# Placing edges into cells: counts on two PSUM banks and ahead of the lookups, drains on VectorE in place of its own semaphores

## The reference, cut to what matters

```python
h = jnp.maximum(_layernorm(x, axis=-1), 0.0)
x = x + _L0_gnn_ref(h, edge_index, edge_attr_40, edge_weight, ...)   # gate MLP, then 4 attention layers
h = jnp.maximum(_layernorm(x, axis=-1), 0.0)
x = x + _L1_gnn_ref(h, edge_index)                                   # 5 steps of spreading over the graph

# in _L0_gnn_ref, on every edge, before the layers:
src, dst = (edge_index[0], edge_index[1])
gate = jax.nn.silu(edge_attr @ F1W + F1b) @ F2W + F2b
msg = gate * h[dst] * (cw * mj)[:, None]
agg = jax.ops.segment_sum(msg, src, num_segments=N)
# in each of the 4 layers: score per edge, segment_max, exp, segment_sum over src
```

## Time and profile before

| what | us |
|---|---|
| median of 3 runs (8886.3 to 8914.17) | 8893.32 |
| the profiled execution, its own time | 8881.17 |
| its span, first to last instruction | 8879.4 |
| first and last start of a scatter in placing | 368.2 and 2786.5 |

### The profile page before, as it was taken

One profiled execution on the slowest core, in us unless ns is written; L12 is line 12 of the kernel. 1 busy time (PEld: TensorE's weight loads), 2 busy tenths in 40 slices (PEclk: granted clock), 3 DMA queues, 4 the chain that ended last, 5 costly groups with the idle time before them and its releaser, 6 DMA issues. The chain is left out here.

```text
span 8879.4 us, 294906 instructions
## 1 busy us (share of the span) xinstructions
PE 6921.8 (78%) x143255; PEld 6085.1 (69%) x89873; DVE 5928.4 (67%) x15778; ACT 4764.3 (54%) x15185; POOL 5505.5 (62%) x7877
## 2 busy tenths in 40 slices
PE   4544454445445999998799979998999989997998
PEld 4433333333334888887588858886888778877998
DVE  5555555555556999998688868876888678873111
ACT  0222222222224888886588858885888768881000
POOL 2266666666666666665588858885888678880000
PEclk9866666666667999999799989997999899998999
DMA  9522222222224777776477737772777457754565
GB/s 390 206 75 74 77 77 74 74 79 77 77 71 125 252 252 247 252 252 212 139 235 236 232 104 234 234 229 96 238 233 237 147 185 236 235 189 198 236 255 210
DMA packets 735820, 1616.56 MB, mean 182 GB/s; under 512 B 97576, under 2 KB 427272, under 8 KB 729955
## 3 DMA queue, kind: packets, MB, share of 16 engines
q1 hardware_dynamic: 674798, 1514.15, 50.9%
q0 software_dynamic: 52768, 77.90, 2.8%
q10 hardware_dynamic: 6869, 5.50, 0.2%
HBM read 1177.09 MB, written 420.09 MB: 180 GB/s over the span
## 5 line engine op out<-in xcount | busy, mean ns | idle before, releaser
L2017 ACT ACTIVATE vals<-carry_h,weight 128x49 f32<-128x49 f32 x9604 | 2322.3, 328 | 6.4
L1013 POOL DMA_INDIRECT edge_records<-rec_space,slot_all x1600 | 1583.4, 990 | 1090.4 <-DVE slot_all L996 554.4
L437 PE MATMUL psum<-TT,hd_t 128*128 128x97 bf16 x9604 | 1380.9, 208 | 120.1 <-POOL ts L2133 68.8
L431 PE MATMUL psum<-TT,hd_t 128*128 128x97 bf16 x19208 | 1445.2, 208 | 0.4 <-issue 0.4
L437 PEld LDWEIGHTS psum<-TT,hd_t 128*128 128x128 fp8e4 x9604 | 938.9, 98 | 422.5 <-DVE carry_h L2131 69.7
L2062 POOL TENSOR_TENSOR vals<-vals 128x343 f32<-128x343 f32 x1372 | 1072.1, 781 | 92.8
L2057 POOL TENSOR_TENSOR vals<-vals 128x343 f32<-128x343 f32 x1372 | 1044.9, 762 | 4.8 <-ACT vals L2017 4.7
L772 ACT COPY attr_t<-psum 80x500 f32<-80x500 f32 x200 | 114.3, 572 | 1538.4 <-remote 1320.1
L1922 DVE SCALAR_TENSOR_TENSOR xks<-recs,psum 128x343 f32<-128x343 f32 x1372 | 695.3, 507 | 343.1 <-PE psum L431 334.5
L431 PE MATMUL psum<-ts,hs_t 128*128 128x49 bf16 x19208 | 922.2, 184 | 0.0
L1894 PE MATMUL psum<-vals,hs 128*128 128x147 bf16 x9604 | 872.6, 234 | 23.8 <-POOL vals L2062 23.7
(11 more groups left out here) (360 smaller groups left out, 15477.8 us busy)
## 6 DMA issues: line engine op xcount, KB each, us to landing
AJ<-adjacency SPq DMA_DIRECT2D x35, 5488.0 KB, 16.7
recs<-attributes SPq DMA_DIRECT2D x196, 686.0 KB, 5.5
hs<-one_hots SPq DMA_DIRECT2D x392, 336.0 KB, 3.1
one_hots<-hots SPq DMA_DIRECT2D x343, 336.0 KB, 4.2
edge_records<-zeros SPq DMA_DIRECT2D x49, 2278.5 KB
recs_g<-edge_records SPq DMA_DIRECT2D x343, 325.5 KB, 5.2
recs<-attributes SPq DMA_DIRECT2D x196, 514.5 KB, 3.7
hd_t<-one_hots SPq DMA_DIRECT2D x196, 448.0 KB, 4.7
```

The source lines that it names most:

```text
L431: return e.add_instruction(mybir.InstMatmult(name=nc.get_next_instruction_name(), engine=mybir.EngineType.PE, ldweights=False, start_tenso ...
L437: e.matmul(out, hot, parts[0], start=True, stop=False)
L1013: e.indirect_dma_start(REC[:, :], bass.IndirectOffsetOnAxis(ap=slot_all[:, i % SR, s:s + 1], axis=0), rec_rings[:, (i // 2) % 4, s, i % 2, ...
L2017: last = e.activation(vals[:, c, 0, :], carry_h[:, par(back), c, :], ACT.Copy, scale=weight[:, par(back), c:c + 1])
```

## The change

The counts of cells go to two PSUM banks in turn (bank 3 for even steps, bank 2 for odd ones). `count(i)` waits for `s_based` of one step earlier than before, and `count(i + 2)` stands at the head of PE's step. On DVE six plain drains a step take the place of the waits on its own semaphores; `s_load` is not posted any more in placing, and the other semaphores are posted as before because other engines or SP wait for them. `move_on` no longer waits for its own `s_based`.

```diff
-                hist_ps = bank(3)[:, 0:8 * NB].rearrange("p (q s b) -> p q s b", q=4, s=2)
+                hist_ps = [bank(3 - r)[:, 0:8 * NB].rearrange("p (q s b) -> p q s b", q=4, s=2) for r in range(2)]
...
                     def count(i):
                         e.wait_ge(s_hot, i + 1)
-                        if i:
-                            e.wait_ge(s_based, i)
+                        if i >= 2:
+                            e.wait_ge(s_based, i - 1)
...
                     for i in range(ITER):
+                        if i + 2 < ITER - 1:
+                            count(i + 2)
                         if i + 1 < ITER:
                             find_bases(i + 1)
                         mlp_step(i + LEAD + 1, "flip", READY)
                         mlp_step(i + LEAD, "hide", READY)
-                        if i + 2 < ITER - 1:
-                            count(i + 2)
                         mlp_step(i + LEAD - 1, "multiply", READY)
...
                             e.wait_ge(s_found, i)
-                            e.wait_ge(s_based, i)
...
                     for i in range(ITER):
-                        e.wait_ge(s_rank, i + 1)
                         e.wait_ge(s_found, i + 1)
-                        e.wait_ge(s_hot, i + 1)
+                        e.drain()
...
                         rank_more(2)
-                        e.wait_ge(s_looked, i + 1)
-                        e.tensor_reduce(found[:, :, :], look[:, :, :, :], AX.X, ALU.add).then_inc(s_load, 1)
+                        e.drain()
+                        e.tensor_reduce(found[:, :, :], look[:, :, :, :], AX.X, ALU.add)
                         rank_more(2)
-                        e.wait_ge(s_load, 4 * i + 2)
-                        e.tensor_tensor(slot_m[:, :], rank[:, i % 2, :], found[:, :, 0], ALU.add).then_inc(s_load, 1)
+                        e.drain()
+                        e.tensor_tensor(slot_m[:, :], rank[:, i % 2, :], found[:, :, 0], ALU.add)
                         rank_more(1)
-                        e.wait_ge(s_load, 4 * i + 3)
+                        e.drain()
```

More of the change, by code:

```diff
@@ L870, in count @@
                         e.wait_ge(s_hot, i + 1)
-                        if i:
-                            e.wait_ge(s_based, i)
+                        if i >= 2:
+                            e.wait_ge(s_based, i - 1)
                         for q in range(4):
-                            last = e.matmul(hist_ps[:, q, :, :].rearrange("p s b -> p (s b)"), pair_of(one_bs, i, q), pair_of(one_bd, i, q), start=True, stop=True)
+                            last = e.matmul(hist_ps[i % 2][:, q, :, :].rearrange("p s b -> p (s b)"), pair_of(one_bs, i, q), pair_of(one_bd, i, q), start=True, stop=True)
                         last.then_inc(s_flat, 1)
@@ L939, in rank_stream @@
                             last.then_inc(s_rank, 1)
-                    e.tensor_copy(mask, lower[:, :]).then_inc(s_load, 1)
+                    e.tensor_copy(mask, lower[:, :])
                     make_hots(0)
@@ L949, in move_on @@
                             e.wait_ge(s_found, i)
-                            e.wait_ge(s_based, i)
                         for s in range(2):
                             spot = lambda r: bases[r % 2][64 * s:64 * s + NB, :, s, 0, :]
-                            last = e.tensor_tensor(spot(i + 1), spot(i), hist_ps[64 * s:64 * s + NB, :, s, :], ALU.add)
+                            last = e.tensor_tensor(spot(i + 1), spot(i), hist_ps[i % 2][64 * s:64 * s + NB, :, s, :], ALU.add)
                         last.then_inc(s_based, 1)
@@ L959, in place_edges @@
                     move_on(0)
-                    e.wait_ge(s_load, 1)
+                    e.drain()
                     for s in range(NS):
@@ L979, in place_edges @@
                         rank_more(2)
-                        e.wait_ge(s_looked, i + 1)
-                        e.tensor_reduce(found[:, :, :], look[:, :, :, :], AX.X, ALU.add).then_inc(s_load, 1)
+                        e.drain()
+                        e.tensor_reduce(found[:, :, :], look[:, :, :, :], AX.X, ALU.add)
                         rank_more(2)
-                        e.wait_ge(s_load, 4 * i + 2)
-                        e.tensor_tensor(slot_m[:, :], rank[:, i % 2, :], found[:, :, 0], ALU.add).then_inc(s_load, 1)
+                        e.drain()
+                        e.tensor_tensor(slot_m[:, :], rank[:, i % 2, :], found[:, :, 0], ALU.add)
                         rank_more(1)
-                        e.wait_ge(s_load, 4 * i + 3)
+                        e.drain()
                         e.scalar_tensor_tensor(slot_a[:, :], slot_m[:, :], float(NB), home[:, i % 3, :], ALU.mult, ALU.add)
-                        e.scalar_tensor_tensor(slot_b[:, :], slot_m[:, :], float(1 - NB), found[:, :, 1], ALU.mult, ALU.add).then_inc(s_load, 1)
+                        e.scalar_tensor_tensor(slot_b[:, :], slot_m[:, :], float(1 - NB), found[:, :, 1], ALU.mult, ALU.add)
                         rank_more(1)
-                        e.wait_ge(s_load, 4 * i + 4)
-                        e.scalar_tensor_tensor(slot_b[:, :], slot_m[:, :], float(CAP), slot_b[:, :], ALU.is_ge, ALU.mult).then_inc(s_load, 1)
+                        e.drain()
+                        e.scalar_tensor_tensor(slot_b[:, :], slot_m[:, :], float(CAP), slot_b[:, :], ALU.is_ge, ALU.mult)
                         rank_more(2)
@@ L994, in place_edges @@
                             scattered(i - SR)
-                        e.wait_ge(s_load, 4 * i + 5)
+                        e.drain()
                         e.tensor_tensor(slot_i[:, i % SR, :], slot_a[:, :], slot_b[:, :], ALU.add).then_inc(s_idx, 1)
```

## The result

| | us |
|---|---|
| before, median of 3 (8886.3 to 8914.17) | 8893.32 |
| after, median of 3 (8830.88 to 8839.14) | 8832.68 |
| ratio, 95% interval | 0.9942, 0.9918 to 0.9966 |
| span of the profiled execution, before and after | 8879.4 and 8830.9 |

The account below looks back on a forecast made before the run. POOL's scatters and its pauses for slots were taken to bound placing. Two thirds of steps at 13.2 us and one third at 11.9 gave 2555 us, +136, hence 9030 us; its own range was 8950 to 9130, the overall one from 8740.

Parts of the forecast that it names:

- What bounds the kernel: Placing: POOL's scatters set a floor of 2080 us; the other 340 us are pauses waiting for slots.
- pattern of cycles: Placing: waits are free about 10 us after POOL restarts, then posts crawl until it pauses, commonly after two steps.
- the flush: Placing: all pending posts land together about 3 us after POOL's last scatter.
- Own waits gone: DVE's slot steps in placing: up to 361 us of idle in 173 steps vanish, 2.1 us a step.
- the third slot at 15 to 16 us: DVE's slot for POOL's third step is ready 15 to 16 us after POOL's restart, so POOL goes on after two steps.
- Six drains at 0.15 us: DVE in placing: drains add 0.9 us a step, exposed only in the look-to-slot chain, five drains, 0.75 us.
- The three-step cycle, 39.7 us: POOL in placing: an early third slot makes three-step runs the rule, 13.2 us a step, with a longer pause after.
- Count first, two banks, 0 with 40 us to either side: PE's count in placing, moved first with two banks: worth 0, with 0.2 us a step (40 us) either way.
- The rival B: Drains wait for pending posts, so the third slot stays at about 20 us: 8893 within some 40 us, chance 0.18.
- two-step cycle: POOL's common run in placing: two steps, then a pause of 2.5 to 3.3 us; 23.1 us, 11.6 us a step.

Follow-up runs that it names:

- posts_kept: The changed kernel with the four s_load posts per step put back, waited for by nobody, drains kept: ratio 0.9955 to the kernel before.
- half_scatters_2: The changed kernel with four scatters a step instead of eight, on a chip where POOL pauses: ratio 0.9129 to the kernel before, placing 1638 us.
- drains_banks_3: The changed kernel with the count back behind the hide, drains and two banks kept, on a chip where POOL pauses: ratio 0.9990 to the kernel before.
- banks_only_2: The kernel before with two count banks and the weaker wait, old count place, own waits kept, on a chip without POOL pauses: ratio 1.0001.
- before_again: The unchanged kernel before, run once more on a chip where POOL pauses: ratio 0.9994, placing 2422 us.
- drains_twice: The changed kernel with each of DVE's six drains per step written twice: ratio 0.9978 to the kernel before, placing 2389 us.
- pool_rest: The changed kernel with a POOL drain and five small fills behind each step's eight scatters, on a chip without POOL pauses: ratio 1.0609, placing 2606 us.

## Why the prediction was wrong

- **What bounds the kernel**: right. POOL's pauses account for 42 of the 45 us in placing; the rest of the kernel is the same within 3 us. The pattern of cycles and the flush about 3 us after POOL's last scatter also stand.
- **"Own waits gone", the third slot at 15 to 16 us**: this is the step that failed. It read 361 us of late posts as the price of posts and took the drain in the late part at its dense price. The third slot came at 22.8 to 23.9 us (10% to 90% of the cycles), since the chain to it took 12.9 us at the median and not 5.2. What is late there is the end of the instruction itself, as a drain sees it; posts_kept shows that posts cost nothing, half_scatters_2 that a drain is short when POOL issues half as many scatters and stands between them. The prediction had said that no drain of the trace stood in the late part, and then gave it a number from outside it.
- **Six drains at 0.15 us**: right in the dense part: 0.17 to 0.18 us each (look to slot 5.3 us for 4.4, look to look 7.8 for 6.7). In the late part they cost 0.5 to 2.2 us each in the cycle shown.
- **The three-step cycle, 39.7 us**: its price was right (the one in the middle of drains_banks_3, with drains, has 1440.06 - 1400.83 = 39.2 us) and its frequency had the wrong sign. Drains slow exactly the chain that would have made the third slot early: of the 5 such cycles with a pause over 6 us none is left. The prediction left the other long pauses out: 12 of the 17 end shorter runs.
- **Count first, two banks, 0 with 40 us to either side**: the size was nearly right and the sign depends on the rest: +30 us with own waits (ratio 1.0034), -48 us with drains (1.0002 to 0.9948). The two parts can't be costed apart.
- **The rival B**, 8893 within 40: the outcome that happened, a third slot no earlier and the two-step cycle kept, with another reason than the one given (the late drains have no post to wait for), and priced without the long pauses. It put the slot at "about 20 us as now" from the one cycle of the earlier trace rows; the median of before is 23.1. It took for granted that with the same two-step cycle the same strays stay; they fell by 76 us in the profiled execution, and 34 us of that came back in the common pauses.

## What to carry to other kernels

A wait's idle time is not what you gain by taking it out; ask what the waiting instruction would stand for next, and look whether the same lateness shows in work that has no such wait. Here a drain and a semaphore were late in the same stretch. In a loop of two engines that lock into a cycle, a change that makes one side slower but regular can win, since each stray late lookup can buy a pause of a whole chain. And measure on more than one chip: the kernel before differed by 350 us between two kinds, and the change is worth 60.

## What the runs showed of the hardware

- The same kernel before takes 8511 us on some chips and 8863 to 8893 on others, and nearly all of it lies in placing (2076 us in banks_only_2 against 2422 in before_again; 13 us lie ahead of it, and what follows takes 6079 us in both). On the slower ones, in the second step of an unbroken run of POOL's scatters, a drain on DVE leaves it idle for 0.5 to 2.2 us more (after, 1465 to 1476 us). With half of the scatters it does not (half_scatters_2). What in the chip makes the difference is open.
- An explicit drain on DVE right behind another lasts 19 ns, and six such drains lengthen a dense step by 0.28 us (drains_twice).
- A scatter that starts 0.05 to 0.2 us behind the start of a DVE comparison of 125x392 elements with a 16-bit result takes 1.31 to 1.33 us and not 0.97 (79 of 79 in banks_only_2); many that start at another moment of it are not stretched.
- A drain on POOL behind eight scatters held it for 1.7 us at the median and 5.1 us at most (pool_rest).
